# Four recurrent layers on one core: groups that end at a half tile, and a 128x128 state between the chunks of the last layer

## What is computed

```
q = xn @ wq ; k = xn @ wk ; v = xn @ wv        # exp(0 * ...) = 1 factors left out
D[i, j] = 0.96875 ** (i - j) for i >= j, else 0   # i, j inside one row of 1024 tokens
s = ((q @ k.T) * D) @ v
```

## Time and profile before

| | us |
|---|---|
| runs | 1001.41, 1002.76 (median), 1005.93 |
| span of the profiled execution | 1003.7 |
| TensorE busy | 920.3 (92%) |
| VectorE busy | 764.0 (76%) |
| GpSimd busy | 597.9 (60%) |
| ScalarE busy | 538.3 (54%) |

### The profile page before, as it was taken

How to read it: one execution, slowest core, us unless ns; L and a number is a source line. 1 busy time by engine, 2 the same in 40 slices (tenths; PEclk the granted TensorE clock), 3 DMA queues, 4 the chain that set the end, 5 groups by cost and what they waited for, 6 DMA issues and landing times. The chain is left out here.

```text
span 1003.7 us, 20954 instructions
## 1 busy us (share of the span) xinstructions
PE 920.3 (92%) x7704; PEld 489.4 (49%) x7713; DVE 764.0 (76%) x1332; ACT 538.3 (54%) x901; POOL 597.9 (60%) x533
## 2 busy tenths in 40 slices
PE   5799997999999999999989997899889787799997
PEld 3346563233333333333323233798788444488794
DVE  6978888888888889887888825883689998873514
ACT  1255345666766666666756775443266243274463
POOL 3660425788778777887777893123735886652333
PEclk9999998999999999999999999799999997999999
DMA  9372525111111101111101123567651200243462
GB/s 319 137 225 88 153 64 156 41 51 46 26 52 28 58 24 49 34 55 56 35 26 44 40 67 116 161 193 241 225 156 35 89 22 22 79 142 101 143 196 79
DMA packets 92308, 97.17 MB, mean 97 GB/s; under 512 B 23184, under 2 KB 68624, under 8 KB 91952
## 3 DMA queue, kind: packets, MB, share of 16 engines
q1 hardware_dynamic: 87088, 85.34, 27.8%
q0 software_dynamic: 5120, 10.50, 3.6%
HBM read 70.57 MB, written 24.77 MB: 95 GB/s over the span
## 5 line engine op out<-in xcount | busy, mean ns | idle before, releaser
L255 PE MATMUL ps<-ar 64*64 64x512 bf16 (+5 forms) x5312 | 538.6, 448 | 17.7 <-ACT ar L301 4.3
L255 PEld LDWEIGHTS ps<-ar 64*64 64x64 bf16 (+2 forms) x5312 | 268.5, 137 | 273.4 <-ACT ar L301 92.0
L277 DVE TENSOR_REDUCE small<-ps 128x2 f32<-128x1024 f32 (+2 forms) x276 | 307.2, 1140 | 52.0 <-PE ps L255 50.6
L301 ACT ACTIVATE ar<-ps 128x1024 f32<-128x1024 f32 (+1 forms) x304 | 285.4, 941 | 113.1 <-PE ps L255 106.5
L264 POOL TENSOR_TENSOR psum_sb<-psum_sb,ar 128x1024 f32<-128x1024 f32 x91 | 214.8, 2360 | 57.3 <-DVE on_sb L264 47.1
L264 POOL TENSOR_TENSOR ar<-ar 128x512 f32<-128x512 f32 (+1 forms) x80 | 79.2, 995 | 52.1 <-DVE ar L277 30.0
L323 POOL DMA_INDIRECT gT<-ysort,rt x48 | 46.9, 977 | 98.7 <-issue 97.7
L264 DVE TENSOR_TENSOR ar<-ps,ar 128x256 f32<-128x256 f32 (+4 forms) x56 | 56.2, 1011 | 47.9 <-PE ps L255 43.4
L264 POOL TENSOR_TENSOR psum_sb<-ar 128x1024 f32<-128x1024 f32 x32 | 75.9, 2372 | 16.8 <-ACT ar L301 15.6
L298 ACT COPY ar<-ps 128x256 f32<-128x256 f32 (+1 forms) x84 | 31.8, 386 | 80.8 <-PE ps L255 50.2
L255 PE MATMUL ps<-wA,xnT 128*128 128x512 f32 (+3 forms) x192 | 62.0, 447 | 5.3 <-DVE ar L264 2.7
(11 more groups left out here) (156 smaller groups left out, 1066.0 us busy)
## 6 DMA issues: line engine op xcount, KB each, us to landing
ar<-in_L_up SPq DMA_DIRECT2D x48, 384.0 KB, 4.1
ar<-in_L_b SPq DMA_DIRECT2D x32, 322.0 KB, 3.4
rec_sb<-lscr SPq DMA_DIRECT2D x64, 128.0 KB
scr<-ar SPq DMA_DIRECT2D x48, 128.0 KB, 2.1
ar<-xsort SPq DMA_DIRECT2D x40, 128.0 KB
ysort<-ar SPq DMA_DIRECT2D x40, 128.0 KB, 3.3
ar<-scr SPq DMA_DIRECT2D x32, 112.0 KB
xsort<-xs SPq DMA_DIRECT2D x12, 256.0 KB, 6.2
```

The lines of the kernel that those rows point to most:

```text
L255: return self.e.matmul(o, l, r, start=start, stop=stop) if self.e else Nothing()
L277: return self.e.tensor_reduce(o, a, AX.X, op, negate=True) if negate else self.e.tensor_reduce(o, a, AX.X, op)
L301: return self.e.activation(o, a, fn, **kw) if self.e else Nothing()
```

## The change

1. `NHALF` keeps the number of half tiles, and a new function `halves(J)` says whether tile J has two or one. Every part of the expert work does only the half tiles that there are, so the last tile of each group has one.
2. In layer 3 a second chunk no longer meets the first's keys and values block by block. A new stage `state3` for c = 0 and 2 makes the keys of the chunk by rows (four 128x128 products), and multiplies them with values that ScalarE has faded by their distance to the chunk's end: a 128x128 state (four more). A second chunk multiplies it once with its faded queries (one product of 128x512, `cross3`) into bank 5. `att3.1` and `att3.3` have 12 steps on TensorE.
3. All lists are new. Two waits are added so that they may differ more (`v` on TensorE for the first weights; VectorE's first sum of a projection for the gathered rows).

The core of the diff:

```diff
-NTG = [((n * 1024 + NE * (HALF - 1)) // HALF + 1) // 2 for n in COPIES]
+NHALF = [(n * 1024 + NE * (HALF - 1)) // HALF for n in COPIES]
+NTG = [(n + 1) // 2 for n in NHALF]
...
+def halves(J):
+    q = max(q for q in range(NG) if FIRST[q] <= J)
+    return min(2, NHALF[q] - 2 * (J - FIRST[q]))
...
-    dt_sb = area(R + 5120, 1024)
+    dt_sb, fade, q_faded, state_sb = (area(R + 5120 + o_, n_) for o_, n_ in ((0, 640), (640, 512), (1152, 512), (1664, 128)))
+    k_rows, v_faded = acc_sb[:, 1536:2048], osb_[:, 512:1024]
...
         def att3(c):
...
+            if hf:
+                pe.wait_ge(*vacant(5))
+                pe.wait_ge(*at("state_sb", c - 1))
+                pe.wait_ge(*at("q_faded", c))
+                pe.mm(ps[:, 5, :], state_sb, q_faded, stop=False).then_inc(*up(("cross3", c)))
+                yield
+            for jb in range(5):
+                if jb < 4:
+                    i0 = 128 * jb
...
+        def state3(c):
+            rows3("k3", "wk", c)
+            yield
+            b = take(ring[0])
+            pe.wait_ge(*vacant(b))
+            pe.wait_ge(*at("k3_sb", c))
+            pe.wait_ge(*at("v_faded", c))
+            for j in range(4):
+                r = slice(128 * j, 128 * j + 128)
+                ins = pe.mm(ps[:, b, 0:128], k_rows[:, r], v_faded[:, r], start=j == 0, stop=j == 3)
+            ins.then_inc(*filled(b, ("state3", c)))
...
-                for k in range(2):
+                for k in range(halves(J)):
                     ins = pe.tr(ps[:, b, 128 * k:128 * k + 128], x_[:, 128 * k:128 * k + 128], ident)
...
+                for j in range(4):
+                    r = slice(128 * j, 128 * j + 128)
+                    act.af(v_faded[:, r], ps[:, bank["v3", c], r], ACT.Copy,
+                           scale=dt_sb[:, 512 - 128 * j:513 - 128 * j]).then_inc(
+                        *(up(("v_faded", c)) if j == 3 else up(("v_faded",))))
...
+        def state3(c):
+            act.wait_ge(*at("k3", c))
...
+            act.acp(k_rows, ps[:, bank["k3", c], :]).then_inc(*emptied(("k3", c), ("k3_sb", c)))
+            yield
+            act.wait_ge(*at("state3", c))
...
+            act.af(state_sb, ps[:, bank["state3", c], 0:128], ACT.Copy, scale=ex).then_inc(
+                *emptied(("state3", c), ("state_sb", c)))
```

Of the lists, TensorE around the end of group 2 and at the end of the program, SP around the last stores of group 2, and GpSimd at the start of layer 2:

```diff
-        "up.2 up.2 xturn.3 down.2 up.3 down.2 xturn.3 up.3 xturn.3 rec.1 rec.1 up.3 up.3 down.3 position xturn.3 "
+        "up.2 xturn.2 down.2 up.2 down.2 up.2 up.2 xturn.2 down.2 up.2 up.2 xturn.2 down.2 up.2 rec.0 position down.2 "
+        "down.2 xturn.3 rec.1 rec.1 xturn.3 up.3 up.3 xturn.3 up.3 up.3 down.3 position xturn.3 xturn.3 up.3 down.3 "
...
-        "down.5 up.5 att3.2 up.5 att3.2 down.5 down.5 att3.2 end3.0 att3.3 att3.3 att3.3 att3.3 att3.3 att3.3 att3.3 "
-        "end3.1 att3.3 att3.3 att3.3 att3.3 att3.3 att3.3 att3.3 att3.3 end3.2 end3.3 "),
+        "up.5 xturn.5 xturn.5 up.5 down.5 up.5 up.5 up.5 down.5 up.5 down.5 down.5 att3.2 end3.0 att3.2 state3.2 "
+        "att3.2 end3.1 att3.2 state3.2 att3.3 att3.3 att3.3 att3.3 att3.3 end3.2 att3.3 att3.3 att3.3 att3.3 end3.3 "),
...
-        "bias.2 store.2 bias.2 store.2 bias.3 store.2 xrows.3 xrows.3 store.2 bias.3 store.2 xrows.3 xrows.3 store.2 "
-        "bias.3 store.2 bias.3 xrows.3 store.3 xrows.3 xrows.3 bias.3 xrows.3 store.3 bias.3 bias.3 bias.3 store.3 "
+        "store.2 store.2 xrows.2 bias.2 bias.3 bias.3 store.2 store.2 xrows.3 xrows.3 bias.3 store.2 store.2 xrows.3 "
+        "xrows.3 xrows.3 bias.3 bias.3 store.3 xrows.3 bias.3 xrows.3 bias.3 xrows.3 store.3 xrows.3 bias.3 store.3 "
...
-        "gather.2 gather.2 ln.2.0 tile.0 tile.0 tile.1 tile.0 tile.0 tile.1 tile.1 tile.1 tile.2 ln.2.1 tile.2 tile.2 "
+        "gather.2 ln.2.0 gather.2 tile.0 tile.1 tile.0 tile.0 tile.1 ln.2.1 tile.1 tile.2 tile.2 tile.3 tile.2 tile.3 "
```

More of the change, by code:

```diff
@@ L532, in _program @@
     lscr = nc.dram_tensor("lscr", [2, 2, 512], F32).ap()
-    xsort = [nc.dram_tensor(f"xsort{h}", [NTG[0] * TILE, 128], F32).ap() for h in range(2)]
-    ysort = [nc.dram_tensor(f"ysort{h}", [NTG[0] * TILE, 128], F32).ap() for h in range(2)]
+    xsort = [nc.dram_tensor(f"xsort{h}", [NHALF[0] * HALF, 128], F32).ap() for h in range(2)]
+    ysort = [nc.dram_tensor(f"ysort{h}", [NHALF[0] * HALF, 128], F32).ap() for h in range(2)]
     rt = sb("rt", [128, 768])
@@ L729, in v @@
             pe.wait_ge(*at("xn", 0, i // 4))
+            pe.wait_ge(*at("wa0_in", 0))
             for hf in range(2):
@@ L981, in tile, with rows3 @@
             ins.then_inc(*filled(b, ("tileT", i)))
+        def rows3(name, w_, c):
+            b = take(ring[0])
+            pe.wait_ge(*vacant(b))
+            for j in range(4):
+                i0 = CW * c + 128 * j
+                ins = pe.mm(ps[:, b, 128 * j:128 * j + 128], xnT[:, i0:i0 + 128], M(w_))
+            ins.then_inc(*filled(b, (name, c)))
         def att3(c):
@@ L992, in att3 @@
                 yield
-            b = take(ring[0])
-            pe.wait_ge(*vacant(b))
-            for j in range(4):
-                i0 = CW * c + 128 * j
-                ins = pe.mm(ps[:, b, 128 * j:128 * j + 128], xnT[:, i0:i0 + 128], M("wv"))
-            ins.then_inc(*filled(b, ("v3", c)))
-            yield
-            for jb in range(nb + 1):
-                if jb < nb:
-                    i0 = max(0, 128 * jb - o_)
+            rows3("v3", "wv", c)
+            yield
+            if hf:
[7 more added lines that the diff above has]
+                    i0 = 128 * jb
                     b = take(ring[0])
@@ L1009, in att3 @@
                 if jb == 1:
-                    pe.wait_ge(*vacant(5))
+                    if not hf:
+                        pe.wait_ge(*vacant(5))
                     pe.wait_ge(*at("v3_sb", c))
@@ L1013, in att3 @@
                     pj = jb - 1
-                    i0 = max(0, 128 * pj - o_)
+                    i0 = 128 * pj
                     pe.wait_ge(*at("decayed", c, pj))
-                    pe.mm(ps[:, 5, i0:512], v3_[:, 128 * pj:128 * pj + 128], scb[pj % 4][:, i0:512], start=pj == 0,
-                          stop=pj == nb - 1).then_inc(
-                        *(filled(5, ("pv3", c, pj)) if pj == nb - 1 else up(("pv3", c, pj))))
+                    pe.mm(ps[:, 5, i0:512], v3_[:, o_ + i0:o_ + i0 + 128], scb[pj][:, i0:512],
+                          start=pj == 0 and not hf, stop=pj == 3).then_inc(
+                        *(filled(5, ("pv3", c, pj)) if pj == 3 else up(("pv3", c, pj))))
                     yield
+        def state3(c):
+            rows3("k3", "wk", c)
+            yield
+            b = take(ring[0])
+            pe.wait_ge(*vacant(b))
+            pe.wait_ge(*at("k3_sb", c))
[4 more added lines that the diff above has]
+            ins.then_inc(*filled(b, ("state3", c)))
         def end3(c):
@@ L1066, in up_ffn @@
             for J in range(FIRST[q], FIRST[q + 1]):
-                for k in range(2):
+                last_k = halves(J) - 1
+                for k in range(last_k + 1):
                     b = 2 * k if layer == 1 else 2 * (J % 2)
@@ L1089, in up_ffn @@
                         numbers_of(J, q)
-                    elif layer == 0 and k and J + 1 < FIRST[q + 1]:
+                    elif layer == 0 and k == last_k and J + 1 < FIRST[q + 1]:
                         numbers_of(J + 1, q)
@@ L1109, in h_turned @@
                         ins = pe.tr(ps[:, b, o + 128 * f:o + 128 * f + 128], h_[:, i0:i0 + 128], ident)
-                    if layer or k:
-                        ins.then_inc(*filled(b, ("hT", J, k)))
+                    if layer or k == halves(J) - 1:
+                        ins.then_inc(*filled(b, ("hT", J, 1)))
                         yield
@@ L1133, in tensor_program @@
                   "end0": end0, "end1": end1, "end2": end2, "tables": tables, "rec": rec, "position": position,
-                  "ffn2": ffn2, "tile": tile, "att3": att3, "end3": end3, "route": route}
+                  "ffn2": ffn2, "tile": tile, "att3": att3, "state3": state3, "end3": end3, "route": route}
         follow(ORDER_A["tensor"], stages)
@@ L1717, in gated @@
             for J in range(FIRST[q], FIRST[q + 1]):
-                for k in range(0 if layer == 1 else 1, 2):
+                for k in range(halves(J)) if layer == 1 else (1,):
                     dve.wait_ge(*at("silu", J, k))
@@ L1916, in att3 @@
         def att3(c):
[L1917 removed]
+            hf = c % 2
+            o_ = 512 * hf
             act.wait_ge(*at("v3", c))
             act.wait_ge(*at("dt_in", 0))
+            if c >= 2:
+                act.wait_ge(*at("pv3", c - 2, 3))
+            if not hf:
+                if c == 2:
+                    act.wait_ge(*at("state3", 0))
+                for j in range(4):
+                    r = slice(128 * j, 128 * j + 128)
+                    act.af(v_faded[:, r], ps[:, bank["v3", c], r], ACT.Copy,
+                           scale=dt_sb[:, 512 - 128 * j:513 - 128 * j]).then_inc(
```

(33 more changed lines are left out.)

80 lines of the change are left out of this document (42 added, 38 removed), and 260 rows, old and new, of tables (ORDER_A, ORDER_C, SIDE_B).

## The result

The changed kernel takes 989.88 us (median of four runs, 985.0 to 991.72) against 1004.35 (four runs, 1001.41 to 1007.15) in the same comparison. The ratio is 0.9851, 95% interval 0.9818 to 0.9884: 14.9 us faster. Run again beside other kernels it came to 0.9851 once more (0.9824 to 0.9878). The forecast was 986, with a range of 977 to 996.

What follows compares the result with a forecast made beforehand. TensorE was taken as the bound except in layer 2, where VectorE is, with two latency chains joining the stages. 1003.7 - 3.3 - 5.5 - 9.2 = 985.7, said as 986 us; range 977 to 996.

Steps and rivals of the forecast that it cites:

- Price of the work: TensorE products and transposes priced start to start; half tiles 3.3, 4.3 and 3.8 us in layers 0, 1 and 3.
- Before the attention, -3.3: Before the attention TensorE is solid, so layer 0's half tiles save 3.3 us; range -6 to +2.
- The attention, 0 within 2: In the attention, 256 steps unchanged and side words only shifted: 0, between -2 and +2 us.
- Start of layer 2: Layer 2 can begin 8.6 us earlier through earlier stores and gathers; -5.5 us taken, ends 0 and -9.
- Rival 1: Layer 2's end doesn't move, as VectorE and group 3's gathers set it: 991.2 us, chance 0.20.
- Layer 3, -9.2: In layer 3, less TensorE work and an earlier sum for the last tile save 9.2 us; between -5 and -11.
- The end: After the last down.5, TensorE's 10.3 us and four hand-overs just fit in 14.6 us, so it stays unchanged.
- Rival 3: Behind the last down.5 the state's chain of hand-overs ends last, at half clock: 989 to 996 us, chance 0.12.
- Rival 4: VectorE's new order in layer 2 meets a tile's exponential too soon, 2.8 us per tile: 1026 us, chance 0.07.
- The rule on the clock: An idle TensorE falls to half clock, so less work may run slower at the end: 989 to 996 us.

Runs made afterwards that it cites:

- e1: Kernel before with only the half tiles left out, all lists old: ratio 0.9960 to the kernel before, 4.0 us faster.
- e2: All of the changed code (half tiles and state) with all lists old: ratio 0.9966 to the kernel before, 3.4 us faster.
- e3: Changed kernel with ORDER_C old, ORDER_A and SIDE_B new: ratio 0.9990 to the kernel before.
- e9: Changed kernel with all lists old except from the attention's end to layer 2's first normalization: ratio 1.0029 to the kernel before.
- e11: Changed kernel with each second chunk's product of state and faded queries done six times instead of once: ratio 0.9925 to the kernel before.
- e10: Changed kernel with old lists until layer 2's first normalization, new order for what is left: ratio 0.9913 to the kernel before.
- e6: Changed kernel with every last tile full again, state and new lists kept: ratio 0.9970 to the kernel before.

## Why the prediction was right, and where not

The total was right (986 forecast, 989.88 measured; 14.9 us gained, 18.0 in the sum). By the profiles three of its terms were each wrong by more than 5 us: the attention (5.7 us longer, 0 forecast), the stretch from its end to the last products (18.2 shorter, 5.5 forecast) and layer 3 (0.2 shorter, 9.2 forecast). Their errors cancelled, and that is luck.

- **Price of the work.** Right in total, under the new lists: 11.4 us for six half tiles, measured 11.9; 8.6 for the ten products in the state's place, measured 7.4. Under the old lists the half tiles bring 4.0 and the state nothing (e1, e2).
- **Before the attention, -3.3.** The half tiles are worth about that: with them put back the first exponential comes at 155.4, without at 151.7 to 152.4. In all it comes 7.8 us sooner, past the end of the range ("From -6 (the exponentials' wait and part of the start go as well)"), since the new list brings 4.3 more (e2 to e3). The first maximum now comes 2.5 us behind the first exponential, since VectorE still clears until 155 (row at 153.24).
- **The attention, 0 within 2.** Wrong: 5.7 us longer in the profile. Six kernels with the new side list have 455.3 to 457.8 us, the others 448.9 to 450.8. TensorE's busy time is the same (437.3 and 436.8), its idle time 12.8 and 19.0. The same words set beside other steps do not take the same time. By the last exponential this leaves 2.2 of the 7.8 us.
- **Start of layer 2.** The chain was right: the gathers start at 694.74 (696.8 forecast), ln.2.0's operation at 712.83 (713 to 716 forecast). What I made of it, -5.5, was too small: 18.2 us go between the attention's end and the last products. I let VectorE keep half of the gain as idle time; its idle time fell by 6.1 us in this stretch (38.1 to 32.0) and by 8.6 in layer 2 besides, where I had seen none to take. Rival 1 was thus wrong for this list, yet e9 shows it at work: layer 2 starts 2.4 us earlier than in e2 and ends 6.6 later.
- **Layer 3, -9.2.** Wrong: 96.9 to 96.7 us. The step that failed is "So the sum can start right at 907, 4.3 sooner" with the 36.7 us of latency behind it. The sum comes no nearer to the last products: it starts 4.6 us behind them before, and in the changed kernel, as the second half of the 32 transposes from 889.14 on, by estimate 4.4 behind their end at 886.46. From the last products to the last scatter 36.7 to 38.3 us pass in every one of the kernels, whatever TensorE's work: the state's saving lies in the shade of this chain. The parts counted as gone ahead of the sum (one down.4, two up.4, one xturn.4, four att3.0) stand behind it in the new list, ahead of the first xturn.5. So each stage hands work on to the next. From e2 to the changed kernel TensorE's records go from 777 to 736 between attention and layer 2, from 855 to 857 in layer 2, and from 258 to 295 between the last products and xturn.5, where e2 has its hole. That is how work taken from layer 3 shows as time ahead of it:

```profile
605.10:719.60 114.50, 102.81 (x777) 90.12 (x769) 76.12 (x242) 42.92 (x107) 38.81 (x43) 0.91 0.61 191
719.60:898.70 179.10, 150.34 (x855) 107.31 (x856) 156.53 (x249) 83.45 (x178) 113.54 (x127) 0.96 0.25 74
```

  From xturn.5 to the last eight gathers 3.3 us went (5.0 forecast), and 2.8 came on top by the sorted rows' later load.
- **The end** stays: 16.5 and 16.8 us. Rival 3 did not come; the last wait is for the gathered rows. With 4.3 us more in it (e11) the end takes 2.8 longer, so by estimate 1.5 us of cover were left.
- **Rival 4** did not come: VectorE's waits of this kind in layer 2 are shorter than before (4.4 us in all, the longest 2.8):

```profile
DVE ar L263 <- ACT ar L300: 1.9, 2, 1.1
```

- **The rule on the clock** was weighed for the end, where the granted clock is 0.90 (0.87 before, stretch from 987.20): nothing was lost. Its example is read loosely: the idle 2.98 us stood ahead of products at 833.21, and the slow sum at 834.89 followed these. The clock changed elsewhere. In the first 30 us after the attention the old order leaves waits in TensorE, and the clock is 0.76 to 0.85 (before, e1, e2, e3, e10). The new order keeps expert parts between the waits, and it is 0.94 to 1.00 in all nine kernels that have it there:

```profile
610.30:640.30 30.00, 20.50 (x134) 12.98 (x127) 24.62 (x103) 8.85 (x22) 5.77 (x10) 0.84 0.43 133
```

```profile
605.10:635.10 30.00, 20.84 (x130) 13.98 (x123) 24.32 (x101) 8.83 (x21) 5.92 (x9) 0.76 0.40 129
```

```profile
608.20:638.20 30.00, 23.59 (x195) 17.08 (x188) 23.64 (x93) 11.07 (x27) 4.23 (x7) 1.00 0.47 149
```

These are the kernel before, all the code with the old lists, and the changed kernel: 134, 130 and 195 records in 30 us. Here the order sets the clock, not the half tiles: e3, with 131 records and the old order behind the attention, has 0.85. The Trainium skill, "TensorE: Matmul & The Clock Gate", section on the HAM clock gate, has it that the idle state is the slow one and that activity releases it; the three rows agree in that the fullest one has the full clock. I had used it only as a danger, and here it may be part of the gain: from the old lists to the new, TensorE's busy time between attention and layer 2 falls by 11.0 us (102.81 to 91.82) for 41 records fewer. How much of that is clock and how much is work moved on was not separated, and e9 has the new order and 0.94 there and is slower all the same.

What stays open: the new lists with all of the old work were not run. By the sum (0.9851 + 0.0119 + 0.0074) they would stand at 1.004, no better than the old ones, if the two costs add. Which words of the side list cost the attention its 6 us was not tried either, nor why the half tiles of layer 1 take more than their price in the profile of e6.

## What to carry to other kernels

Where engines follow fixed lists, judge work and lists together: here the smaller work under the old lists brought 3.4 us, with one half of the new list it was slower than before, and with all of it it brought 15. Before pricing work that is removed, look for the chain of latencies beside it (last products to last scatter, 36.7 to 38.3 us in fourteen profiles) and ask which other work the lists can move into its shade. The time appears where that work came from, not where the removed work was. And when one engine only issues DMAs, read its list as a queue: whatever delays a buffer delays the loads that stand behind it.

## What the runs showed of the hardware

SP's issue of four weight loads takes 2.79 us with 644 columns a row and 2.78 with 132: here the time goes by the load, not by its bytes. A single profiled execution stood up to 5.2 us from its kernel's median (e9: 1001.76 against 1006.96), so differences between two spans of less than that say little unless a stage repeats them.
